# First attention of a four-block kernel: shift rows written by DMA instead of added by select matmuls, odd head moved to a step's begin

## The chip, the cores and the metric
The kernel runs on one core of a Trainium2 chip. The metric is the device time in microseconds of the whole program, the median over several executions.

## What is computed
The reference is a chain of six stages over 2048 tokens of 128 channels (8 sequences of 256): mixture of experts, attention, mixture, and once more in a second layer. The change touches the first attention alone:

```python
qkv = (x @ w_qkv.T + b_qkv).reshape(b, n, 3, H, D).transpose(2, 0, 3, 1, 4)   # H = 16, D = 8
q, k = elu(q) + 1.0, elu(k) + 1.0
q, k = _apply_rope(q, sin, cos), _apply_rope(k, sin, cos)
attn = softmax(einsum("bhnd,bhmd->bhnm", q, k) * scale, axis=-1)
out = einsum("bhnm,bhmd->bhnd", attn, v) + lepe   # lepe: a convolution of v over 3 tokens
```

With 8 sequences, 16 heads and 256 queries, each softmax row has 256 keys.

## The kernel before
**Stages.** The stages f0 (mixture), a0 (the attention of this case), g0, f1, a1 and g1 follow one another with a barrier of all engines at each stage's end (stage_end in build). In each stage every engine has a program of its own, written out by hand: sync for SP, gpsimd for POOL, tensor for PE, scalar for ACT, vector for DVE.

**Scores twice.** [...] By query (scores_by_query, L2069, and scores_by_query_paired, L2081): queries on partitions, 256 keys along the free dimension, two halves of 128 queries into one PSUM bank; DVE takes the negated maximum of it (maximum, L2292). By key (scores_by_key, L2106): keys on partitions, queries along the free dimension, into banks 2 to 5; ACT takes the exponential of two heads at once (probabilities, L2240). The negated maximum of a query has to be added to each by-key score before that.

**How it is added before.** Queries and keys are kept as a high part and a rest (three rows of 8 values = 24 rows, PARTS), and a head has 32 partitions (HW) of the turned tiles, four heads to a tile. The negated maxima of a batch are split into a bf16 high part and a rest (split_maxima, L2300), turned by PE (turn_maxima, L2096) and copied by DVE (take_shift, L2309) into a tile shift of 128 partitions. After a by-key matmul of 24 rows a second matmul of 32 rows with the 0/1 tile select adds them into the same bank.

**Order.** A batch (one sequence) has 8 steps of two heads, step n = 8 b + u. In step n PE does the by-key scores of the step's pair, and the by-query scores of the pair three steps later (LEAD = 3). The order of one step on PE: by-key of both heads, by-query of the even head, the product with V of four heads (values, in odd steps), turning of the output (turn_out, in even steps), the projection of V with its convolution (u = 5), turning of stacks (u = 1 to 4), turn_maxima (u = 6), projection of a later batch (u = 7), and at last by-query of the odd head. On DVE: split_maxima (u = 5), take_shift (u = 7), maximum of the even head, elu, finish, take_out, maximum of the odd head. Before step 0 there are 11 steps without by-key scores, and most of these do both heads in scores_by_query_paired. The last 11 steps have no by-query scores. The fp32 bank 7 (T) is used in turn by turnings of stacks, the convolution, the projection and the maxima; claim(7) waits for its last reader.

**SP in this stage.** The attention's own sync is empty. In build, SP's block then runs, for a0, fills.sync (L506: two transfers from the tile empty into the slot tables of the later mixtures, then a wait for both) and write_pads (L350: six transfers of the tile pad into z, then a wait for all).

Of the kernel before, what the change touches and what calls it, by code (L numbers as in the profile page):

```python
# [23 lines left out]
P = 128  # L24
# [377 lines left out]
class Ahead:  # L402
# [9 lines left out]
    def place(self, ctx, w):  # L412
# [9 lines left out]
        self.head = sb("head", [P, H0], BF16)  # L422
        self.select = sb("select", [P, H0, P], BF16)
# [23 lines left out]
    def constants(self, pool):  # L447
        pool.memset(self.ones_f[:, :], 1.0)
        pool.memset(self.edge[:, :, :], 0.0)
        pool.memset(self.bias_rows[:, :, :], 0.0)  # L450
        self.step(pool, pool.memset(self.head[:, :], 0.0))
# [1377 lines left out]
def attention_zero(core, name, ctx, w):  # L1829
# [11 lines left out]
    PARTS = 3 * D0  # L1841
    STEPS = H0 // 2
# [6 lines left out]
    wqkv, wv, cos, sin, ones_f, bias_rows, edge, select = (ahead.wqkv, ahead.wv, ahead.cos, ahead.sin, ahead.ones_f,  # L1849
                                                          ahead.bias_rows, ahead.edge, ahead.select)  # L1850
# [8 lines left out]
    mparts = sb("mparts", [P, 2, 4, 2 * H0], BF16)  # L1859
    shift = [sb(f"shift{i}", [P, SEQ], BF16) for i in range(2)]  # L1860
# [25 lines left out]
    shift_ready = sem("shift_ready")  # L1886
    s2_done = sem("s2_done")
# [38 lines left out]

    def group_of(n, lag):

        return (n - lag) // 2 if (n - lag) % 2 == 0 and 0 <= (n - lag) // 2 < BATCH * GROUPS else None
# [16 lines left out]
    def sync(sp):  # L1946
        pass
# [30 lines left out]
    def gpsimd(pool):  # L1978
# [6 lines left out]
        for m in stack:  # L1985
            pool.memset(m[:, :, :, :, PARTS:HW].rearrange("p a t h d -> p (a t h) d"), 0.0).then_inc(filled, 1)
# [22 lines left out]
    def tensor(pe):  # L2009
# [20 lines left out]
        def turn_stack(b, v):  # L2030
# [4 lines left out]
            if b == 0 and v == 0:  # L2035
                pe.wait_ge(filled, 3)
# [32 lines left out]
        def scores_by_query(b, h):  # L2069
            n, g, rows = b * H0 + h, h // HG, slice(HW * (h % HG), HW * (h % HG) + PARTS)  # L2070
            if h % (2 * HG) == 0:
                pe.wait_ge(tk_ready, 4 * b + 2 * (h // (2 * HG)) + 2)
            if n >= 2:
                pe.wait_ge(max_done, n - 1)
            q, k = turned[b % NT]
            for t in range(2):
                last = pe.matmul(bank[h % 2][:, SEQ * t:SEQ * t + SEQ], q[rows, g, P * t:P * t + P].bitcast(F32R),  # L2077
                                 k[rows, g, :].bitcast(F32R), start=True, stop=True)
            last.then_inc(s1_done, 1)
# [16 lines left out]
        def turn_maxima(b):  # L2096
            claim(T)
            pe.wait_ge(parts_ready, b + 1)
            for t in range(2):
                last = pe.transpose(bank[T].bitcast(BF16)[:, P * t:P * t + P],  # L2100
                                    mparts[:, t, :, :].rearrange("p i h -> p (i h)"), core.identb[:, :])
# [933 lines left out]
```

## Time and profile before

| | us |
|---|---|
| median of 3 runs | 1029.71 |
| the runs | 1030.68, 1021.74, 1029.71 |
| the profiled execution | 1020.3 |
| its span, first to last instruction | 1018.5 |
| PE busy in the span | 862.1 (85%) |
| DVE busy | 749.3 (74%) |
| ACT busy | 520.8 (51%) |

The first attention takes the stretch from about 131 to 313 us of the span. A row of the timeline gives the start, the duration, the engine, the line, the operation, the tile written and the tile read, and the number of instructions merged in the row; in brackets, the idle time before and what ended it. Windows give busy time per engine in a stretch.

### The profile page before, as it was taken

The numbers are of one execution on the slowest core, as the hardware profiler recorded it, in microseconds if no ns is written. First come the engines' busy times: TensorE is split into PE (matmuls) and PEld (weight loads), VectorE is DVE, ScalarE is ACT, GpSimd is POOL, SyncE is SP. The second block draws the span as 40 slices with busy tenths as digits, with TensorE's granted clock in tenths as the row PEclk, the third lists the DMA queues.
The fourth block names the chain that finished last, engine by engine and source line by source line (L and its number), as shares of the span: only waits on it lengthen the run. The fifth ranks groups of instructions, "written<-read, shape, count | busy, mean of one in ns | idle before, by whom it ended". The sixth has DMA issues, their size and how long they took to land.

```text
span 1018.5 us, 23321 instructions
## 1 busy us (share of the span) xinstructions
PE 862.1 (85%) x7492; PEld 655.8 (64%) x7492; DVE 749.3 (74%) x2654; ACT 520.8 (51%) x1365; POOL 284.5 (28%) x395
## 2 busy tenths in 40 slices
PE   4899989999996899945999188999999998548992
PEld 3457856667765457833999166677767776437992
DVE  7758888788767866877577658877787778566675
ACT  4233044666564223014465238877887788434653
POOL 3034035634001003117755180001000000077741
PEclk9999995999996999965899679999999999859996
DMA  9204079810006304056231256645454552343313
GB/s 238 71 1 141 1 280 374 264 52 2 2 1 161 80 1 141 1 168 187 80 84 34 84 147 194 185 123 159 149 174 139 157 155 84 92 143 90 104 36 125
DMA packets 134947, 119.74 MB, mean 118 GB/s; under 512 B 10755, under 2 KB 115227, under 8 KB 134836
## 3 DMA queue, kind: packets, MB, share of 16 engines
q1 hardware_dynamic: 130292, 109.83, 36.4%
q0 software_dynamic: 4544, 8.54, 2.5%
q8 instruction: 57, 0.93, 0.4%
q14 instruction: 54, 0.44, 0.1%
HBM read 67.45 MB, written 51.80 MB: 117 GB/s over the span
## 4 chain that ended last, share of the span: by engine, by line
PE 63%; DVE 16%; ACT 12%; issue 4%; DMA 3%; DVEq 1%; SPq 0%; POOL 0%; POOLq 0%; ACTq 0%
PE psum L955 7%; PE psum L964 6%; PE psum L1551 6%; PE psum L1465 5%; ACT a_L L2799 3%; ACT a_L L2797 3%; PE psum L2139 3%; PE psum L2669 3%; PE psum L2718 3%; PE psum L2077 3%; PE psum L2705 2%; PE psum L2042 2%; PE psum L743 2%; PE psum L1491 2%; ACT a_PT L2808 2%
## 5 line engine op out<-in xcount | busy, mean ns | idle before, releaser
L2297 DVE TENSOR_REDUCE a_negmax<-psum 128x2 f32<-128x512 f32 x128 | 83.7, 684 | 20.9 <-PE psum L2077 19.5
L2246 ACT ACTIVATE a_PT<-psum 128x1024 f32<-128x1024 f32 x64 | 65.5, 1023 | 26.2 <-PE psum L2122 25.8
L2799 ACT ACTIVATE a_L<-a_L,a_least 128x256 f32<-128x256 f32 x128 | 63.3, 495 | 0.0
L1010 ACT ACTIVATE f_hT<-psum,f_wt 128x128 f32<-128x128 f32 x156 | 44.5, 369 | 36.5 <-PE psum L955 36.5
L1010 ACT ACTIVATE g_hT<-psum,g_wt 128x128 f32<-128x128 f32 x156 | 44.4, 370 | 33.3 <-PE psum L955 33.3
L2669 PE MATMUL psum<-a_KT,a_Q 64*128 64x128 f32 (+1 forms) x512 | 57.6, 342 | 3.3 <-DVE a_least L2859 0.9
L2797 ACT ACTIVATE a_L<-a_L,a_least 128x128 f32<-128x128 f32 x128 | 50.6, 395 | 10.7 <-DVE a_least L2859 9.8
L2857 DVE CUSTOM_DVE_ANT_0 a_L<-psum,a_X 128x128 f32<-128x128 f32 x128 | 36.6, 286 | 25.0 <-PE psum L2669 24.9
L2116 PE MATMUL psum<-a_turned 24*128 24x256 f32 x256 | 53.8, 359 | 0.0
L2859 DVE CUSTOM_DVE_ANT_0 a_L<-psum,a_X 128x256 f32<-128x256 f32 x128 | 53.7, 420 | 0.0
L2808 ACT ACTIVATE a_PT<-psum 128x768 f32<-128x768 f32 x64 | 51.2, 800 | 1.7 <-PE psum L2685 0.9
L2077 PE MATMUL psum<-a_turned 24*128 24x256 f32 x224 | 51.3, 338 | 0.9 <-ACT a_turned L2212 0.7
L2685 PEld LDWEIGHTS psum<-ident,a_L 64*128 64x128 f32 x768 | 30.6, 139 | 30.7 <-ACT a_PT L2808 17.5
L2705 PE MATMUL psum<-a_PT,a_V 128*64 128x256 f32 (+1 forms) x512 | 49.9, 338 | 0.0
L163 POOL MEMSET g_logit<- 128x128 f32 x1 | 0.2, 204 | 170.7 <-DVEq L2937 170.7
L896 POOL DMA_INDIRECT g_back_dram<-g_y,g_xin x39 | 40.3, 1033 | 25.0 <-DVE g_y L1093 20.7
L896 POOL DMA_INDIRECT f_back_dram<-f_y,f_xin x39 | 39.6, 1015 | 27.5 <-DVE f_y L1093 23.6
L2122 PE MATMUL psum<-a_shift,ahead_select 32*128 32x256 bf16 x256 | 47.2, 289 | 0.0
L955 PE MATMUL psum<-f_xT,f_wt 128*128 128x128 f32 x312 | 43.4, 284 | 3.2 <-DVE f_xT L1087 3.2
L2705 PEld LDWEIGHTS psum<-a_PT,a_V 128*64 128x64 f32 x512 | 32.4, 139 | 19.7 <-issue 10.5
L2600 DVE TENSOR_SCALAR a_L<-a_L,a_rinv 128x256 f32<-128x256 f32 x128 | 44.5, 348 | 0.0
L955 PE MATMUL psum<-g_xT,g_wt 128*128 128x128 f32 x312 | 41.3, 276 | 1.9 <-DVE g_xT L1087 1.9
(579 smaller groups left out, 2563.3 us busy)
## 6 DMA issues: line engine op xcount, KB each, us to landing
z<-a_G SPq DMA_DIRECT2D x32, 512.0 KB, 3.5
a_X<-z SPq DMA_DIRECT2D x16, 1024.0 KB, 6.7
f_slots_dram<-empty SPq DMA_DIRECT2D x1, 8910.0 KB, 28.1
g_slots_dram<-empty SPq DMA_DIRECT2D x1, 8910.0 KB, 51.6
a_X<-z SPq DMA_DIRECT2D x16, 512.0 KB, 4.1
f_wgu<-in_gate_up SPq DMA_DIRECT2D x16, 384.0 KB, 6.6
z<-pad SPq DMA_DIRECT2D x6, 1024.0 KB, 9.7
g_wgu<-in_gate_up SPq DMA_DIRECT2D x16, 384.0 KB, 6.5
```

Source lines behind the costliest of these rows:

```text
L896: pool.indirect_dma_start(back_dram[:, :], bass.IndirectOffsetOnAxis(ap=xin[:, i, P:P + 1].bitcast(I32), axis=0), y[i % YBUF][:, :], None, ...
L955: last = pe.matmul(bank[i % 2][:, P * c:P * c + P], wt[i % WBUF][:, P * c:P * c + P], xT[:, i % 2, :], start=True, stop=True)
L964: last = pe.matmul(bank[4 + i % 2][:, 0:P], hT[:, i % 2, c, :], wt[i % WBUF][:, OUT + P * c:OUT + P * c + P], start=(c == 0), stop=(c == F ...
L1010: act.activation(hT[:, i % 2, c, :], bank[i % 2][:, P * c:P * c + P], ACT.Relu, bias=wt[i % WBUF][:, B1 + c:B1 + c + 1]).then_inc(relu_don ...
L2077: last = pe.matmul(bank[h % 2][:, SEQ * t:SEQ * t + SEQ], q[rows, g, P * t:P * t + P].bitcast(F32R), k[rows, g, :].bitcast(F32R), start=Tr ...
L2246: act.activation(PT[m % 4][:, :, :, :].rearrange("p j t n -> p j (t n)"), core.psum[:, 2 + 2 * (u % 2):4 + 2 * (u % 2), :], ACT.Exp, scale ...
L2297: dve.tensor_reduce(negmax[:, :, h], query_bank(b, h).rearrange("p (t n) -> p t n", n=SEQ), AX.X, ALU.max, negate=True).then_inc(max_done, 1)
L2669: last = pe.matmul(out, Q[rows, at, b % 2, queries], KT[rows, at, b % 2, keys], start=True, stop=True)
L2705: last = pe.matmul(o[D1 * i:D1 * i + D1, queries], V[s][:, kt, D1 * h:D1 * h + D1], PT[:, (2 * m + i) % TSLOTS, keys], start=(kt == 0), st ...
L2797: act.activation(pr[:, o, 0:P], L[:, o, 0:P], ACT.Exp, bias=least[:, o, 0:1], scale=-1.0, accum_out=sums[:, o, 0:1])
L2799: act.activation(pr[:, o, P:3 * P], L[:, o, P:3 * P], ACT.Exp, bias=least[:, o, 1:2], scale=-1.0, accum_out=sums[:, o, 1:2]).then_inc(p_re ...
L2808: act.activation(own.rearrange("p (k r c) -> p r k c", r=2, c=HP), core.psum[:, 2:4, 0:3 * P].rearrange("p r (k c) -> p r k c", c=HP), ACT ...
```

## The change
The select tile and its constants go. The turned queries get two more rows in use per head: rows 24 and 25 of each head's 32 hold the high part and the rest of the negated maximum, and the same rows of the keys' stack are filled with 1.0, so the by-key matmul of 26 rows adds them by itself. The rows are written by SP with eight DMAs per batch, out of a tile shift of 32 partitions in fp32r. The attention's sync now stands behind fills.sync and write_pads in SP's program. The by-query scores of the odd head are now begun at a step's begin, interleaved by halves with the by-key scores, and both maxima stand together on DVE. The turning of the maxima moves from u = 6 to 5, take_shift from the begin of u = 7 to the end of u = 5, and values_and_convolution from u = 5 to 6.

```diff
-        groups = self.head[:, :].rearrange("p (g j) -> p g j", j=HG)
-        for part in range(2):
-            self.step(pool, pool.affine_select(out=groups, in_=groups, compare_op=ALU.not_equal, fill=1.0, base=-H0 * part,
-                                               pattern=[[-HG, H0 // HG], [-33, HG]], channel_multiplier=1))
-        pool.tensor_copy(self.select[:, :, :], bcast(self.head[:, :], P))
...
-    mparts = sb("mparts", [P, 2, 4, 2 * H0], BF16)
-    shift = [sb(f"shift{i}", [P, SEQ], BF16) for i in range(2)]
+    mparts = sb("mparts", [P, 2, 2 * H0])
+    shift = [sb(f"shift{i}", [2 * H0, SEQ]) for i in range(2)]
...
-        return i + 1 if u == 5 and 1 < i + 1 < BATCH else None
+        return i + 1 if u == 6 and 1 < i + 1 < BATCH else None
...
     def sync(sp):
-        pass
+
+        for b in range(BATCH):
+            sp.wait_ge(shift_ready, b + 1)
+            for part in range(2):
+                for g in range(GROUPS):
+                    s = H0 * part + HG * g
+                    sp.dma_start(turned[b % NT][0][PARTS + part::HW, g, :],
+                                 shift[b % 2][s:s + HG, :]).then_inc(rows_written, 16)
...
-            pool.memset(m[:, :, :, :, PARTS:HW].rearrange("p a t h d -> p (a t h) d"), 0.0).then_inc(filled, 1)
+            pool.memset(m[:, 0, :, :, PARTS:HW].rearrange("p t h d -> p (t h) d"), 0.0).then_inc(filled, 1)
+            pool.memset(m[:, 1, :, :, PARTS:SHIFTED].rearrange("p t h d -> p (t h) d"), 1.0).then_inc(filled, 1)
+            pool.memset(m[:, 1, :, :, SHIFTED:HW].rearrange("p t h d -> p (t h) d"), 0.0).then_inc(filled, 1)
...
-        def scores_by_key(b, u):
+        def scores(b, u, second):
             m = b * STEPS + u
+            if second:
+                place_for_query(*second, second_order(*second))
+                by_query(*second, 0)
             if u == 0:
-                pe.wait_ge(shift_ready, b + 1)
+                pe.wait_ge(rows_written, WRITES * (b + 1))
             if m >= 2:
                 pe.wait_ge(p_ready, m - 1)
-            q, k = turned[b % NT]
             for t in range(2):
+                if second and t:
+                    by_query(*second, 1)
                 for j in range(2):
-                    h = 2 * u + j
-                    rows = slice(HW * (h % HG), HW * (h % HG) + PARTS)
-                    pe.matmul(bank[2 + 2 * (u % 2) + j][:, SEQ * t:SEQ * t + SEQ],
-                              k[rows, h // HG, P * t:P * t + P].bitcast(F32R), q[rows, h // HG, :].bitcast(F32R),
-                              start=True, stop=False, skip_group_check=True)
-                for j in range(2):
-                    h = 2 * u + j
-                    rows = slice(HW * (h % HG), HW * (h % HG) + HW)
-                    last = pe.matmul(bank[2 + 2 * (u % 2) + j][:, SEQ * t:SEQ * t + SEQ], select[rows, h, :],
-                                     shift[b % 2][rows, :], start=False, stop=True, skip_group_check=True)
+                    last = by_key(b, u, j, t)
             last.then_inc(s2_done, 1)
...
                 if n == 0:
-                    pe.wait_ge(max_done, H0 + 4)
-                scores_by_key(i, u)
+                    pe.wait_ge(max_done, H0 + 6)
+                scores(i, u, due[1])
...
-            if u == 6 and inside(i + 1):
+            if u == 5 and inside(i + 1):
                 turn_maxima(i + 1)
...
-            if due[1] and n not in PAIRED:
-                scores_by_query(*due[1])
+            if due[1] and n < PAIRED.start:
+                scores_by_query(*due[1], H0 * due[1][0] + due[1][1])
...
-            if due[0]:
-                maximum(*due[0])
+            if due[0] and n < 0:
+                maximum(*due[0], H0 * due[0][0] + due[0][1])
+            elif due[0]:
+                maximum(*due[1], second_order(*due[1]))
+                maximum(*due[0], first_order(*due[0]))
...
+            if u == 5 and inside(i + 1):
+                take_shift(i + 1)
...
             for n, st in enumerate(made):
-                st["sync"](sp)
                 if names[n] == "a0":
                     fills.sync(sp)
                     core.early.write_pads(sp)
+                st["sync"](sp)
```

Here by_query and by_key issue one matmul each (a half of 128 queries or keys, 256 columns), by_key with 26 rows; place_for_query holds the waits that scores_by_query had. first_order and second_order number the maxima in the new order (odd head first).

## Rows read from the trace of the kernel before

**Rows 1.** The page, the granted TensorE clock in 40 slices (tenths).
```profile
PEclk9999995999996999965899679999999999859996
```
**Rows 2.** Windows over the stage: window, length; busy PE, PEld, DVE, ACT, POOL; PEclk; DMA share; GB/s.
```profile
149.00:163.90 14.90, 12.88 (x72) 8.82 (x70) 13.91 (x25) 5.29 (x9) 12.16 (x19) 0.70 1.02 372
163.90:176.50 12.60, 12.60 (x88) 9.10 (x86) 9.93 (x31) 5.89 (x7) 4.03 (x15) 0.54 1.02 374
176.50:189.00 12.50, 11.81 (x133) 8.14 (x134) 10.81 (x27) 8.33 (x11) 12.27 (x17) 1.00 0.75 254
...
209.00:229.00 20.00, 19.24 (x216) 13.85 (x208) 16.16 (x39) 11.87 (x15) 7.11 (x12) 1.00 0.01 3
...
267.00:285.00 18.00, 17.68 (x210) 12.72 (x202) 14.61 (x37) 10.68 (x14) 0.00 (x0) 1.00 0.01 2
```
**Rows 3.** Timeline of SP, the time it spends on issuing DMAs.
```profile
132.31 0.68 SPq L510 DMA_DIRECT2D f_slots_dram<-empty  x1
133.04 15.67 SPq L510 DMA_DIRECT2D g_slots_dram<-empty  x1
184.71 18.11 SPq L356 DMA_DIRECT2D z<-pad  x6
...
465.83 1.41 SPq L385 DMA_DIRECT2D early_bnd<-in_b_nd  x4
```
**Rows 4.** What SP waited for, 110 to 310 us: total, times, longest.
```profile
SPq L2951 <- DMA z<-pad: 6.0, 1, 6.0
```
**Rows 5.** Timeline of PE: a pair of heads, first by-key scores, two blocks.
```profile
152.80 0.50 PE L2090 MATMUL psum<-a_turned 24*128 24x256 f32 x4
...
163.89 0.58 PE L2116 MATMUL psum<-a_turned 24*128 24x256 f32 x2
...
272.03 0.38 PE L2077 MATMUL psum<-a_turned 24*128 24x256 f32 x1
...
272.25 0.27 PE L2077 MATMUL psum<-a_turned 24*128 24x256 f32 x1
...
272.94 0.44 PE L2146 MATMUL psum<-ident,a_OT 128*128 128x128 f32 x2
...
305.55 0.39 PE L2116 MATMUL psum<-a_turned 24*128 24x256 f32 x2
...
306.24 0.44 PE L2146 MATMUL psum<-ident,a_OT 128*128 128x128 f32 x2
```
**Rows 6.** DMA issues by line: count, KB each, us from issue to landing.
```profile
g_slots_dram<-empty SPq DMA_DIRECT2D x1, 8910.0 KB, 51.6
...
z<-pad SPq DMA_DIRECT2D x6, 1024.0 KB, 9.7
...
f_wg<-in_Wg SPq DMA_DIRECT2D x1, 4.0 KB, 1.6
```
**Rows 7.** Windows at the stage's start, columns as in rows 2.
```profile
131.00:132.00 1.00, 0.53 (x2) 0.26 (x3) 0.68 (x4) 0.20 (x1) 0.52 (x1) 0.56 0.00 0
...
134.00:136.00 2.00, 1.30 (x6) 0.40 (x4) 1.70 (x10) 0.00 (x0) 0.00 (x0) 0.87 1.00 366
```
**Rows 8.** Timeline of PE and DVE, steps 5 to 7 of a late batch.
```profile
273.75 0.38 PE L2077 MATMUL psum<-a_turned 24*128 24x256 f32 x1
...
275.38 0.29 DVE L2307 TENSOR_TENSOR a_mparts<-a_negmax,a_mparts 128x128 bf16<-128x128 f32 x1
275.78 0.69 DVE L2297 TENSOR_REDUCE a_negmax<-psum 128x2 f32<-128x512 f32 x1
276.39 0.41 DVE L2327 COPY a_OT<-psum 128x256 f32<-128x256 f32 x1
...
281.33 0.28 DVE L2314 COPY a_shift<-psum 128x256 bf16<-128x256 bf16 x1
...
281.76 0.38 PE L2077 MATMUL psum<-a_turned 24*128 24x256 f32 x1
```
**Rows 9.** Timeline of POOL after the constants of the first mixture.
```profile
65.43 0.30 POOL L462 COPY ahead_wv<-ahead_wqkv 128x128 f32<-128x128 f32 x1 [56.09 <-PE psum L1438]
```

More of the change, by code:

```diff
@@ L1841, in attention_zero @@
     PARTS = 3 * D0
+    SHIFTED = PARTS + 2
     STEPS = H0 // 2
@@ L1847, in attention_zero @@
     T, VB = 7, 6
-    wqkv, wv, cos, sin, ones_f, bias_rows, edge, select = (ahead.wqkv, ahead.wv, ahead.cos, ahead.sin, ahead.ones_f,
-                                                          ahead.bias_rows, ahead.edge, ahead.select)
+    wqkv, wv, cos, sin, ones_f, bias_rows, edge = (ahead.wqkv, ahead.wv, ahead.cos, ahead.sin, ahead.ones_f,
+                                                  ahead.bias_rows, ahead.edge)
     e = [sb(f"e{i}", [P, 4, P]) for i in range(2)]
@@ L1886, in attention_zero @@
     shift_ready = sem("shift_ready")
+    rows_written = sem("rows_written")
     s2_done = sem("s2_done")
@@ L1925, in query_bank, with second_order, first_order @@
         return bank[(3, 5)[h % 2]] if n in PAIRED and n % 2 == 0 else bank[h % 2]
+    def second_order(b, h):
+        n = b * H0 + h
+        return n - 1
+    def first_order(b, h):
+        n = b * H0 + h
+        return n if (n // 2 - STEPS - LEAD) < 0 else n + 1
     def group_of(n, lag):
@@ L2067, in values_and_convolution, with place_for_query, by_query, by_key @@
             release[i] = (l_added, b + 1)
-        def scores_by_query(b, h):
-            n, g, rows = b * H0 + h, h // HG, slice(HW * (h % HG), HW * (h % HG) + PARTS)
-            if h % (2 * HG) == 0:
+        def place_for_query(b, h, order):
+            if h % (2 * HG) in (0, 1):
                 pe.wait_ge(tk_ready, 4 * b + 2 * (h // (2 * HG)) + 2)
-            if n >= 2:
-                pe.wait_ge(max_done, n - 1)
+            if order >= 2:
+                pe.wait_ge(max_done, order - 1)
+        def by_query(b, h, t):
+            g, rows = h // HG, slice(HW * (h % HG), HW * (h % HG) + PARTS)
             q, k = turned[b % NT]
+            last = pe.matmul(bank[h % 2][:, SEQ * t:SEQ * t + SEQ], q[rows, g, P * t:P * t + P].bitcast(F32R),
+                             k[rows, g, :].bitcast(F32R), start=True, stop=True)
+            if t:
+                last.then_inc(s1_done, 1)
+        def by_key(b, u, j, t):
+            h = 2 * u + j
+            g, rows = h // HG, slice(HW * (h % HG), HW * (h % HG) + SHIFTED)
+            q, k = turned[b % NT]
+            return pe.matmul(bank[2 + 2 * (u % 2) + j][:, SEQ * t:SEQ * t + SEQ], k[rows, g, P * t:P * t + P].bitcast(F32R),
+                             q[rows, g, :].bitcast(F32R), start=True, stop=True)
+        def scores_by_query(b, h, order):
+            place_for_query(b, h, order)
             for t in range(2):
-                last = pe.matmul(bank[h % 2][:, SEQ * t:SEQ * t + SEQ], q[rows, g, P * t:P * t + P].bitcast(F32R),
-                                 k[rows, g, :].bitcast(F32R), start=True, stop=True)
-            last.then_inc(s1_done, 1)
+                by_query(b, h, t)
         def scores_by_query_paired(b, h):
@@ L2290, in elus, with maximum @@
                                      ALU.add).then_inc(elu_ready, 1)
-        def maximum(b, h):
-            n = b * H0 + h
-            dve.wait_ge(s1_done, n + 1)
-            if h == 0 and b:
+        def maximum(b, h, order):
+            dve.wait_ge(s1_done, order + 1)
+            if h in (0, 1) and b:
                 dve.wait_ge(parts_ready, b)
@@ L2312, in take_shift @@
             if b >= 2:
-                dve.wait_ge(s2_done, STEPS * (b - 1))
-            dve.tensor_copy(shift[b % 2][:, :], bank[T].bitcast(BF16)[:, 0:SEQ]).then_inc(shift_ready, 1)
+                dve.wait_ge(rows_written, WRITES * (b - 1))
+            dve.tensor_copy(shift[b % 2][:, :].bitcast(F32R), bank[T][0:2 * H0, 0:SEQ]).then_inc(shift_ready, 1)
         def add_convolution(b):
@@ L2372, in vector @@
                 add_convolution(value_step(n - 1))
-            if u == 7 and inside(i + 1):
-                take_shift(i + 1)
-            if due[0]:
-                maximum(*due[0])
+            if due[0] and n < 0:
[3 more added lines that the diff above has]
+                maximum(*due[0], first_order(*due[0]))
             if n in (-6, 0):
@@ L2384, in vector @@
                 take_out(group_of(n, 3))
-            if due[1]:
-                maximum(*due[1])
+            if due[1] and n < 0:
+                maximum(*due[1], H0 * due[1][0] + due[1][1])
+            if u == 5 and inside(i + 1):
+                take_shift(i + 1)
     return dict(sync=sync, gpsimd=gpsimd, tensor=tensor, scalar=scalar, vector=vector)
```

21 lines of the change are left out of this document (8 added, 13 removed).

## The prediction
> **What bounds the kernel now.** I read the profile from coarse to fine. The 40 slices (25.5 us each) come first: the granted TensorE clock is at 0.9 of full speed or more in most, and at 0.5 in the seventh, 153 to 178 us, which belongs to this stage [rows 1]. The windows over the stage come second [rows 2]. They say that the stage, 131 to 313 us, is carried by PE: it is busy 19.24 of 20.0 us in an early batch (209 to 229) and 17.68 of 18.0 in a late one (267 to 285). DVE is next, with 16.16 of 20.0 and 14.61 of 18.0. So an edit that frees PE gains at once, but only until DVE, 2 to 3 us per batch behind, takes over. The same windows hold what decides this case: from 149 to 189 us, and on until the pads have landed, the 16 DMA engines are full (share 1.02 until 176.5, then 0.75 with the gap at 184 in it, 254 to 374 GB/s), and after 209 they are empty. Third, SP's own timeline and waits [rows 3, 4]. In the kernel before SP has nothing to do for the attention, so it sends the two fills at 132.31 and 133.04, waits until the second has landed (133.04 + 51.6 = 184.6 [rows 6]), sends the six pads until 202.8, and waits 6.0 us for them. Nobody waits for SP in this, since the stage runs to 313 us. Fourth, the block of the scores on PE, instruction by instruction [rows 5].
>
> **The changed place of SP's work: the stall.** The first scores by key begin at 163.89 us [rows 5]. In the changed kernel they need the shift rows written by DMA (step 0 of PE waits on rows_written), and these DMAs stand in SP's program behind fills.sync and write_pads, each of which ends with a wait for its own transfers. SP is free at 184.71 + 18.11 + 6.0 = 208.8 us [rows 3, 4]. Nothing in the change makes the fills shorter: they move 2 x 8.9 MB and 6 x 1 MB through full engines [rows 2, 6]. Then come eight DMAs of 4 KB. SP issued four small ones (5 KB each) in 1.41 us, 0.35 each [rows 3]; the eighth starts 7 x 0.35 = 2.5 us after the first. A lone 4 KB load landed 1.6 us after its issue [rows 6]. With 0.1 for SP to come out of its wait: 208.8 + 0.1 + 2.5 + 1.6 = 213.0 us. **The first step is late by 213.0 - 163.9 = 49.1 us.** Bounds: nothing shows an SBUF to SBUF transfer. Large issues take 0.47 each and the fill's rate could differ by 1 us, so 48 to 52.
>
> Does other work fill the stall? Behind the waiting PE stands everything of the attention. Before it waits, PE does one matmul of a by-query score; the second half of it comes after the first by-key matmuls, so s1_done does not rise, the maximum on DVE waits, behind it DVE's statistics and the elu of batch 3, and so POOL. ACT waits for s2_done. Nothing that is on the path later can be done early, so I subtract nothing. The barrier at the stage's end moves the rest of the program by the same time.
>
> **Clock after the stall.** Behind the barrier at the stage's start, where PE was busy for 0.53 of 1 us, the clock was 0.56, and 3 us later 0.87; from 163.9 to 176.5 it was 0.54, although PE was busy throughout [rows 2, 7]. [...] I take 0. [...]
>
> **The additions by select.** A step's block before: four by-query matmuls (two heads, two halves), four by key, four by select. It ran from 272.03 to 272.94 = 0.91 us [rows 5]. Without queries, as in the last 11 steps, four by key and four by select took 306.24 - 305.55 = 0.69 us [rows 5]. Four matmuls of 24 rows in two row groups showed 0.50 us from start to end [rows 5], with the second pair 0.22 behind the first and some 0.28 of latency; so the pitch of one row group is 0.22 and the pair costs 0.44. The changed block has eight matmuls in four row groups: odd query and two keys together, then their second halves at 0.22, and the even head's two, which can start beside them at 0.22 and 0.44: 0.66 us. If only two row groups ran at once it would be 4 x 0.22 = 0.88; if all four did it would be 0.44. I take 0.66, because the block before also holds more than two at a time. Saved: 0.25 per step with queries, 0.69 - 0.44 = 0.25 per step without. [...]
>
> There are 53 steps with queries: 53 x 0.25 = 13 us. DVE limits it: a maximum takes 0.69 us, 0.6 behind one another, two per step [rows 8], and a late batch has 14.61 us of DVE in 18.0, with little slack in the steps that have no turning of stacks. I count three quarters: 10 us (bounds 2 and 18). The 11 last steps: 11 x 0.25 = 2.7 us, nothing else binds there.
>
> **The rows of batches 1 to 7.** The split now stands with the turning in step 5 and the result must be in place at step 8. Take a late batch, step 5 beginning at 273.75 [rows 8]. The split ended at 275.67 (+1.9). DVE then does two maxima (1.2), the copy of O (0.4) and take_shift (0.3): +3.8 [rows 8]. Eight DMAs: +2.5, landing +1.6: +7.9. The next batch began at 281.76, +8.0 [rows 8]; with three shorter blocks PE would be there at +7.3. So a wait of 0.6 us in three late batches (the others have a projection in step 7), 2 us together; at 0.47 an issue and 2.5 us of landing it would be up to 1.8 in seven, 12 us. This DMA chain is why steps 5 to 7 gain almost nothing in the late batches. What is queued behind: the convolution of step 6 claims bank 7, which take_shift frees at +3.8; the split at 128x128 and the bf16 copy get smaller operands, less than 0.5 us per batch of DVE, counted with the three quarters.
>
> **Small edits.** Head and select vanish from POOL's constants in the first mixture, where POOL afterwards idles 56 us before its next piece [rows 9]: 0. Four more memsets and the wait at H0 + 6 lie ahead of step 0 and are covered by the stall: 0. Without that cover the wait would cost one maximum, 0.7.
>
> **Sum.** 1020.3 + 49.1 (stall) - 10 - 2.7 (blocks) + 2 (rows) + 0 (clock) = 1058.7 us, against the profiled execution. Its 1020.3 stands 9.4 below the median of three runs; the four executions shown average 1025.6. I put the same +38.4 on that: 1064 us.
>
> **Rivals.**
> - *Rows become a chain of their own* (7 in 100): issue and landing at their upper bounds, so each batch waits 1.8 us and half the blocks' gain goes: 1025.6 + 51 - 6 + 12 = 1083. For it: the slack of 0 in the late batches. Against: small DMAs show 0.35 and 1.6.
> - *The whole gain comes through* (20 in 100, among the 92 of the forecast): block at 0.44, DVE no limit: 53 x 0.47 x 0.75 = 19, so 1025.6 + 49 - 19 - 2.7 + 1 = 1054.
> - *Faster, since step 0 isn't held* (1 in 100): it decides from the moment SP is free by about 170 us, for then stall and gain cancel. The price of the stall would be 0 and the time 1025.6 - 10.7 = 1015. It needs the fills and pads, 24 MB, to be through 39 us sooner; the rows show the engines full, so nothing speaks for it except that SP's waits are read from code.
> - *The change does little*: stall and gain both small, within 1% (2 in 100): SP would have to be free near 175 to 185 us.
>
> **How the numbers follow.** The forecast with its variants (92 in 100) gives 1064, with its own range from 1025.6 + 48 - 21 - 2.7 = 1050 to about 1080 (stall 52, blocks 5, rows 6, clock +2). The range 1050 to 1082 leaves out the slow tail of the first rival and the two small ones. One per cent is about what a measurement of this kernel can tell from no change: slower by over that 0.96, within 0.02, faster 0.02.
>
> **What the profile after should show.** SP's eight DMAs of batch 0 begin at about 209 us and PE and DVE are empty from 164 to 213; no matmul reads select; the block takes 0.66 us; the stage from resumption to barrier is near 149 - 11 = 138 us against 149. Wrong would be: DMAs of the rows before 200 us, a block of 0.88, or PE waiting more than 1 us for rows in each batch.

## The result, and the profile after

The changed kernel takes 1078.62 us (median of 4 runs, 1076.05 to 1081.36) against 1028.61 for the kernel before (4 runs): a ratio of 1.0506, 95% interval 1.0458 to 1.0554. It is 50 us slower; 38 were forecast.

The stall is where the forecast put it. SP's timeline of the changed kernel (start, duration; the last row is from a narrower window):

```profile
131.63 0.68 SPq L502 DMA_DIRECT2D f_slots_dram<-empty  x1
132.37 15.68 SPq L502 DMA_DIRECT2D g_slots_dram<-empty  x1
183.10 17.29 SPq L356 DMA_DIRECT2D z<-pad  x6
...
206.84 4.52 SPq L1957 DMA_DIRECT2D a_turned<-a_shift  x8
```

They answer [rows 3]. The fills and pads run as before, and the first row DMA of the attention is issued at 206.84 us, although the maxima of batch 0 were ready some 45 us earlier. The chain of work that ended last, between 205 and 216 us (start, duration, what):

```profile
196.76 10.06 DMA z<-pad
...
206.84 0.68 SPq L1957
...
210.87 1.62 DMA a_turned<-a_shift
...
212.53 0.58 PE psum L2102 x2
```

The first by-key matmul, at 163.89 us in [rows 5], stands at 212.53. PE's waits say it too (total, times, longest):

```profile
PE psum L2102 <- DMA a_turned<-a_shift: 47.8, 4, 45.2
```

One wait of 45.2 us, and 2.6 us over three later ones (3.9 over six if PE's weight loads are counted, the longest 1.3). So once SP is free the eight small DMAs cost each batch little.

What follows the stall was expected to be shorter than before and is longer. From the first by-key matmul to the next stage's first DMA (312.91 us before, 372.97 after) it is 149.0 us before and 160.5 after. Windows of the changed kernel over that stretch (window, length; busy PE, PEld, DVE, ACT, POOL; granted clock; DMA share; GB/s):

```profile
212.50:225.50 13.00, 11.87 (x73) 7.93 (x73) 9.19 (x27) 6.91 (x8) 5.96 (x17) 0.50 0.00 1
225.50:250.00 24.50, 20.67 (x194) 11.96 (x192) 18.10 (x43) 13.65 (x18) 16.71 (x24) 0.86 0.01 2
250.00:338.60 88.60, 81.05 (x767) 52.19 (x766) 68.72 (x162) 48.24 (x62) 21.11 (x30) 0.92 0.01 3
338.60:355.80 17.20, 16.57 (x111) 9.82 (x111) 9.54 (x27) 6.23 (x7) 0.00 (x0) 0.51 0.01 3
355.80:373.00 17.20, 13.27 (x149) 7.05 (x147) 6.92 (x25) 10.75 (x12) 0.00 (x0) 1.00 0.01 2
```

The column to read is the clock, 1.00 in both late rows of [rows 2] (209 to 229 and 267 to 285). Here it is 0.50 for the first 13 us, 0.51 for 17 us in the last batch, and 0.92 in between. In windows of 1 us it is at 1.00 or at 0.50, but for those in which it changes; the two are called full clock and lower level from here on. The 0.92 is made of short falls of 3 to 4 us, one at each batch's begin, such as this one:

```profile
300.00:301.00 1.00, 0.54 (x8) 0.43 (x12) 0.93 (x3) 0.47 (x1) 0.98 (x1) 0.84 0.00 0
301.00:302.00 1.00, 1.00 (x12) 0.27 (x4) 1.00 (x3) 0.00 (x0) 1.00 (x2) 0.50 0.00 0
302.00:303.00 1.00, 1.00 (x8) 0.72 (x4) 0.90 (x2) 0.00 (x0) 0.92 (x3) 0.50 0.00 0
303.00:304.00 1.00, 1.00 (x11) 0.57 (x9) 0.00 (x0) 0.60 (x1) 1.00 (x1) 0.50 0.00 0
304.00:305.00 1.00, 1.00 (x11) 0.83 (x12) 0.97 (x2) 0.92 (x2) 0.94 (x3) 0.95 0.00 0
```

Counted in windows of 1 us, the clock is at the lower level for some 51 us between the first and the last by-key matmul, against 12 in the kernel before. The blocks of the scores, where nothing holds them up, are shorter than forecast. PE's timeline of two blocks of the changed kernel, and DVE's row just before the even head's pair of the first:

```profile
288.68 0.39 PE L2102 MATMUL psum<-a_turned 26*128 26x256 f32 x2
...
289.27 0.47 PE L2093 MATMUL psum<-a_turned 24*128 24x256 f32 x2
289.67 1.07 PE L2162 MATMUL psum<-a_PT,a_Vs 128*32 128x256 f32 x16
...
294.53 0.38 PE L2093 MATMUL psum<-a_turned 24*128 24x256 f32 x1
294.54 0.39 PE L2102 MATMUL psum<-a_turned 26*128 26x256 f32 x2
294.55 0.48 PE L2093 MATMUL psum<-a_turned 24*128 24x256 f32 x2
...
294.98 1.07 PE L2162 MATMUL psum<-a_PT,a_Vs 128*32 128x256 f32 x16
```
```profile
287.84 1.29 DVE L2319 TENSOR_REDUCE a_negmax<-psum 128x2 f32<-128x512 f32 x2 [0.48 <-PE psum L2093]
```

The second block, with all eight matmuls in four row groups, takes 294.98 - 294.53 = 0.45 us. The first takes 0.99: the even head's pair starts at 289.27, 0.59 behind the others. The only wait that place_for_query leaves open there is that for DVE's maxima, and DVE's two maxima end at 287.84 + 1.29 = 289.13, just before; so the delay is DVE's. The profile itself names no releaser there.

The short block isn't the usual one. Of 39 blocks with queries between 243 and 338 us (from a block's first matmul to PE's next other matmul, clock 0.92 on average) 12 took 0.44 to 0.45 us, 15 took 0.95 to 1.07, and 5, in the first two steps of a batch, 1.56 to 1.93. The mean is 0.88. In the kernel before, 48 blocks between 176 and 288 us had a mean of 0.97, and 37 of them took 0.91 to 0.93.

### The profile page after: what moved, and what is told of

It reads as the page before. It is cut to its first block, busy times and chain, and to the rows that moved or that the text cites. A ratio compares the mean times of both kernels' runs of the same rounds, so it can differ in the third digit from the quotient of the medians.

```text
span 1074.3 us, 22893 instructions
## 1 busy us (share of the span) xinstructions
PE 862.0 (80%) x7236; PEld 643.0 (60%) x7236; DVE 750.7 (70%) x2654; ACT 518.3 (48%) x1365; POOL 283.7 (26%) x395
## 4 chain that ended last, share of the span: by engine, by line
PE 52%; DVE 15%; ACT 13%; issue 5%; SPq 5%; DMA 4%; another core or an unknown queue 3%; POOL 1%; DVEq 1%; POOLq 0%; ACTq 0%
PE psum L947 6%; PE psum L956 6%; PE psum L1543 5%; PE psum L1457 4%; ACT a_L L2822 3%; ACT a_L L2820 3%; PE psum L2162 3%; PE psum L2741 3%; PE psum L2692 3%; PE psum L2093 2%; ACT a_PT L2831 2%; PE psum L2728 2%; PE psum L1483 2%; SPq L502 2%
## 5 line engine op out<-in xcount | busy, mean ns | idle before, releaser
L2102 PE MATMUL psum<-a_turned 26*128 26x256 f32 x256 | 36.3, 366 | 47.8 <-DMA a_turned<-a_shift 47.8
L2820 ACT ACTIVATE a_L<-a_L,a_least 128x128 f32<-128x128 f32 x128 | 50.6, 396 | 10.7 <-DVE a_least L2882 9.8
L2102 PEld LDWEIGHTS psum<-a_turned 26*128 26x128 f32 x256 | 21.9, 211 | 52.1 <-DMA a_turned<-a_shift 49.4
L2093 PE MATMUL psum<-a_turned 24*128 24x256 f32 x224 | 46.8, 365 | 7.7 <-DVE a_negmax L2319 5.3
L2162 PE MATMUL psum<-a_PT,a_Vs 128*32 128x256 f32 x512 | 41.8, 452 | 3.5 <-DVE a_attn L2357 2.1
L2093 PEld LDWEIGHTS psum<-a_turned 24*128 24x128 f32 x224 | 29.1, 211 | 25.8 <-issue 13.5
## 6 DMA issues: line engine op xcount, KB each, us to landing
z<-pad SPq DMA_DIRECT2D x6, 1024.0 KB, 10.1
```

What stands on the lines that cost most here:

```text
L2162: last = pe.matmul(bank[VB][VW * j:VW * j + VW, 0:SEQ], Vs[b % NT][:, t, HG * g + j, :], PT[(2 * m + j // 2) % 4][:, j % 2, t, :], start=( ...
L2820: act.activation(pr[:, o, 0:P], L[:, o, 0:P], ACT.Exp, bias=least[:, o, 0:1], scale=-1.0, accum_out=sums[:, o, 0:1])
```

## The measure used from here on

The experiments change both the work of the stretch and the clock during it. To tell the two apart I multiply the stretch from the first to the last by-key matmul by its mean granted clock. The product is an estimate of mine: the length at a granted clock of 1.00 throughout, if PE set the pace everywhere and its pace went with the clock. (PE is busy for 0.89 to 0.97 of the stretch; the idle rest is counted at the same mean clock, so the product is a measure of PE's work and its waits together.) How far it holds is seen where the work is the same: the two traces of the kernel before, at clocks of 0.96 and 0.90, come to 137.4 and 138.3 us (below). The kernel before, then the changed one:

```profile
163.90:307.00 143.10, 139.41 (x1502) 98.74 (x1500) 110.83 (x278) 85.27 (x103) 43.68 (x70) 0.96 0.29 95
```
```profile
212.50:367.00 154.50, 140.25 (x1245) 87.55 (x1245) 109.86 (x271) 83.24 (x103) 43.79 (x70) 0.84 0.01 3
```

143.1 x 0.96 = 137.4 us before, 154.5 x 0.84 = 129.8 us after. The clock is given to two digits, so the product is good to 0.8 us. Each product rests on one profiled execution.

The same rows, by the same estimate, give PE's busy time alone at full clock: 139.4 x 0.96 = 133.8 us before, 140.25 x 0.84 = 117.8 after, so 16 us of work have gone. But PE is idle for 14.3 us of the stretch instead of 3.7. Most of the difference between the 16 us and the 7.6 by which the products differ is this idle time.

## The experiments

The experiments ran on four chips, on each beside the kernel before. The chips differed by up to 4%: the kernel before took 1066.55 us (median) on the chip of the first four runs, 1025.89 on that of the next four, 1068.14 on that of the next three (fillers ahead of step 0) and again 1068.14 on that of the last one (the order alone). Whole times are therefore compared only as ratios to the kernel before on the same chip. The difference between the chips lies behind this stage: from the next stage's first DMA to the end it is 701 to 708 us in the six traces of the faster chips and 738 to 745 in the eight of the slower ones. Stretches inside the stage can be compared across chips.

### Is the place of SP's work the whole stall?

**Rows first.** The attention's sync stands ahead of the fills again:

```diff
             for n, st in enumerate(made):
+                st["sync"](sp)
                 if names[n] == "a0":
                     fills.sync(sp)
                     core.early.write_pads(sp)
-                st["sync"](sp)
```

> The changed kernel with the attention's own sync ahead of the fills and pads again, so that the rows of batch 0 can be written at about 161 us; the fills and pads (24 MB) then come after the last rows, near the stage's end. Theory S (the place of SP's work is the whole stall): the first by-key matmuls come at about 166 us instead of 212.5, PE is never idle for more than 4 us, and the attention's last PE instruction comes at 166 + 150..160 = 316 to 326 us; then the barrier waits for fills and pads, some 76 us, so the whole time is 1020 + 75 + 0..12 = 1095 to 1110. Rival (the rows are late for a reason of their own, contention or the transfer itself): the first by-key matmuls later than 175 us. For the rest of the loss: if it is only the clock after the 48 us gap, the stretch from first by-key matmul to last PE instruction falls from 160 to 149 or less; if it is the order and the waits for rows, it stays above 152.

Measured, in one execution: first by-key matmul at 167.8 us, 1131.48 us in all. SP's timeline of this run shows the rows from 162.06 us and the fills after them, at the stage's end:

```profile
162.06 150.83 SPq L1957 DMA_DIRECT2D a_turned<-a_shift  x64
312.94 0.66 SPq L502 DMA_DIRECT2D f_slots_dram<-empty  x1
313.64 16.05 SPq L502 DMA_DIRECT2D g_slots_dram<-empty  x1
```

So 44.7 of the 48.6 us come from the place in SP's program. The other 3.9 (2.5 against the second trace of the kernel before, below) remain with SP free: from the first of the eight DMAs to the first by-key matmul it is 5.7 us. The whole time was above the expected 1095 to 1110, but on a slower chip, which adds some 35 us behind the stage. The second question has an answer as well: the stretch is 155.5 us long (167.8 to 323.3), as long as after a 48 us gap, at a mean clock of 0.81. So the lower clock of this stretch isn't a consequence of the gap.

**Rows by ACT.** The rows of batches 0 to 2 are issued from ACT's own queue, and SP does fills and pads first:

```diff
+    BY_ACT = 3
...
+        for b in range(BY_ACT, BATCH):
+            write_rows(sp, b)
...
                 probabilities(i, u)
+            if u == 6 and 0 <= i + 1 < BY_ACT:
+                write_rows(act, i + 1)
```

> The changed kernel with the rows of batches 0, 1 and 2 issued by ACT (its own DMA queue, behind its work of step 6), SP keeps fills and pads first and the rows of batches 3 to 7. Theory S: the stall goes, the first by-key matmuls come at 166 to 170 us, the whole time is 1078.6 - 46 + 2..6 (ACT busy with issuing eight DMAs in batches 1 and 2, rows landing between the packets of the fills) = 1033 to 1040, near or a little above the kernel before. Rival 1 (the rows queue behind the fills whatever engine issues them, since the 16 DMA engines are full): first by-key matmuls at 184 us or later, time above 1050. Rival 2 (once the stall is gone the removal of select shows its gain): below 1020.

Measured: ratio 1.0222 (1.0192 to 1.0251), first by-key matmul at 179.3 us. That is between the theory and its first rival, and the trace shows a third thing. ACT's timeline while the fills and pads are under way (the rows at 164 and 198 us, DMA share 1.02 and 0.94), and after them (225 us, share 0.03):

```profile
164.41 10.14 ACTq L1955 DMA_DIRECT2D a_turned<-a_shift  x8
174.60 0.60 ACT L2240 ACTIVATE a_turned<-psum 128x512 fp32r<-128x512 f32 x1 [9.60 <-issue]
...
198.19 9.22 ACTq L1955 DMA_DIRECT2D a_turned<-a_shift  x8
...
225.34 4.58 ACTq L1955 DMA_DIRECT2D a_turned<-a_shift  x8
```

Issuing the eight DMAs took 10.1 and 9.2 us at those shares and 4.6 at 0.03, and ACT's other work stands behind it. The last row DMA of batch 0 was issued by 174.6 us, the first by-key matmul came 4.8 us later. So the rows didn't wait for the end of the fills (184 us), but they were slow (3.5 us of PE's wait for batch 0, 4.6 for batch 1) and held up their issuer; after the first one PE waits for rows 7.5 us more, over four waits, against 2.6 in the changed kernel.

**Dealt out.** SP does rows of batch 0, a quarter of the fills, rows of batch 1, the next quarter, and so on; the pads follow the rows of batches 4 and 5, and all waits stand at the end:

```diff
+                    core.fill_part = lambda sp, b: (fills.part(sp, b) if b < 4 else
+                                                    core.early.write_some(sp, b - 4) if b < 6 else None)
                 st["sync"](sp)
+                if names[n] == "a0":
+                    fills.wait_all(sp)
+                    core.early.wait_pads(sp)
```

> The changed kernel with SP's order dealt out: rows of batch 0, a quarter of the two fills, rows of batch 1, the next quarter, and so on, three pads behind the rows of batches 4 and 5 each, all waits for fills and pads at the end. Theory S (the place of SP's work is the stall): first by-key matmuls at 166 to 168 us, no long gap, whole time 45 to 49 us below the changed kernel on the same chip, so a ratio of 1.000 to 1.010 to the kernel before. The forecast's step on the blocks (11 us gained): ratio 0.990. Theory C (the clock): in this kernel too some 50 us of the attention at the lower clock against 20 before, and from the first by-key matmul to the stage's end 153 to 162 us.

Measured: ratio 1.0119 (1.0075 to 1.0163). First by-key matmul at 168.8 us. This removes 38.7 thousandths of the 50.6, some 40 us (the two intervals leave 33 to 46). Theory S said 45 to 49; in the traces the first by-key matmul comes 43.7 us earlier than in the changed kernel. Some 10 us are left (1.0119; medians 1035.1 against 1025.89). Of these 3.5 to 4.9 are still the rows' own way, by which the first by-key matmul is later than in the two traces of the kernel before (163.9 and 165.3); the rest must lie behind it. The stretch, from this kernel's windows:

```profile
168.80:318.00 149.20, 135.65 (x1242) 85.42 (x1241) 109.83 (x271) 82.50 (x103) 43.77 (x70) 0.87 0.48 167
```

149.2 x 0.87 = 129.8, the same as in the changed kernel, with 39 us at the lower clock. Theory C had expected some 50, and 153 to 162 us to the stage's end; it was 155.6.

### Does the clock after the stall matter?

**Warm stall.** PE computes on ones while it would wait:

```diff
+                if n == 0:
+                    for _ in range(215):
+                        pe.matmul(bank[2], core.ones[:, :], some, start=True, stop=True)
                 scores(i, u, due[1])
```

> The changed kernel with 215 matmuls of ones (128x512, bf16) on PE, into a bank that is free, while it would wait for the rows of batch 0: 46 us of work at the higher clock in a gap of 48. Theory C (the cold clock after the stall costs most of what the forecast missed, about 11 us in batch 0): granted clock 1.0 at the first by-key matmuls, batch 0 shorter by 6 to 11 us, whole time 1067 to 1073 against 1078.6. Rival (the clock is low for what the steps themselves do, whatever came before): the clock falls again within batch 0, gain 0 to 3 us, time 1075 to 1079.

Measured: ratio 1.0527 (1.0495 to 1.0558), not below the 1.0506 of the changed kernel. The windows show that the filler did what it should (213 fillers in 45.0 us, 0.21 us each), and that it was no use:

```profile
175.00:220.00 45.00, 43.56 (x213) 20.00 (x211) 2.88 (x8) 2.42 (x3) 0.00 (x0) 1.00 0.65 204
220.00:222.00 2.00, 1.46 (x9) 1.15 (x10) 1.93 (x12) 0.81 (x2) 0.00 (x0) 0.50 0.00 0
222.00:238.00 16.00, 15.19 (x102) 8.69 (x106) 10.61 (x25) 7.94 (x10) 14.38 (x29) 0.50 0.01 3
```

Clock 1.00 for 45 us of fillers, and 0.50 from some 4 us after the by-key steps begin (216.5 us), for some 20 us (the rows show 18). By-key steps began 4.0 us later than in the changed kernel, so the stretch is what counts, and it is no shorter: 156.1 us against 154.5. The rival stands as far as this goes: keeping PE busy beforehand didn't keep the clock up in the steps. What in the steps lets it fall, the run doesn't say. 156.1 x 0.83 = 129.6.

### Is it the clock that takes the blocks' gain away?

**The kernel before again.**

> The kernel before, unchanged, for its trace on the same chip as the next three. [...]

I expected what the first trace shows: one low stretch of some 20 us, and 149 us from the first by-key matmul to the stage's end. That was wrong, and usefully so. One execution gave 159.9 us from the first by-key matmul to the stage's end (165.3 to 325.2). The same code has a second low stretch here, from 190 to 210 us:

```profile
189.00:209.00 20.00, 19.31 (x133) 12.19 (x132) 11.61 (x25) 8.90 (x11) 7.59 (x11) 0.54 0.95 285
```

Where the first trace shows 220 matmuls in this window at clock 1.00, this one has 133 at 0.54. The run took 1031.45 us, 11 more than the first profiled execution. From the first by-key matmul to the stage's end the difference is 159.9 - 149.0 = 10.9 us. So 20 us more at the lower level cost 10.9 us in one and the same kernel, and it is at least one cause of the spread of the kernel before between 1021 and 1031. By the product, 153.7 x 0.90 = 138.3: the same work as in the first trace.

**One and two fillers a step.** Dealt out as above, with matmuls that compute nothing at the begin of each step (one, and six at a batch's first step; then two and eight):

```diff
+            if m >= 2:
+                pe.wait_ge(p_ready, m - 1)
+                for _ in range(6 if u == 0 else 1):
+                    pe.matmul(bank[2 + 2 * (u % 2)], core.ones[:, :], some, start=True, stop=True)
```

> e5_dealt_out with matmuls that compute nothing: one of 128x512 bf16 at the begin of each step, six at each batch's first step, ahead of the wait for the rows. They add 64 x 0.21 + 8 x 1.1 = 22 us of work to PE. Theory C (the clock falls because PE has less work in its steps once select is gone, and each fall costs more than the work saved): fewer than 25 us at the lower clock, the stretch 4 to 10 us shorter than in e5, although PE does more. Rival (PE and DVE time alone decide): the same or up to 10 us longer than e5.

> As e6_filler_one with two at each step and eight at a batch's first: 64 x 0.43 + 8 x 1.3 = 38 us of work added. Theory C: the clock is high throughout after the first steps; the time as e6 or up to 5 us above it, since PE is then full. Rival: 15 to 25 us above e5.

Measured: ratios 1.0096 (1.0058 to 1.0133) and 1.0145 (1.0101 to 1.0188). The stretches, first with one filler a step, then with two:

```profile
168.90:319.00 150.10, 141.88 (x1340) 86.15 (x1340) 109.10 (x271) 85.55 (x103) 43.69 (x70) 0.96 0.48 166
```
```profile
168.00:325.60 157.60, 151.06 (x1411) 88.51 (x1411) 110.30 (x273) 86.02 (x103) 43.76 (x70) 0.98 0.46 158
```

The clock part of theory C holds: all falls after 180 us are gone (clock 1.00 from 181 us to the stretch's end in both), 12 and 7 us at the lower level instead of 39. The time part holds by half: the stretch with 14 us more of work in it (150.1 x 0.96 = 144.1 against 129.8) lasts 150.1 us against 149.2. It isn't shorter by the 4 to 10 us expected. What the clock gives back the filler eats; the intervals of the whole-time ratios 1.0119 and 1.0096 overlap. With two fillers the stretch is 7.5 us longer than with one and 8.4 longer than without, between theory C (0 to 5 above one) and its rival (15 to 25 above none). The expectations counted 22 and 38 us of filler; the products rise by 14 and 25, so part of the filler went into time in which PE was idle.

### Can the first low stretch be prevented?

The kernel before and two of the above, with three fillers in each of the eight steps ahead of step 0; "dealt out" also with five at a batch's first step:

```diff
+                for _ in range(3):
+                    pe.matmul(bank[T if n < -4 else 4], core.ones[:, :], some, start=True, stop=True)
```

> The kernel before, with three matmuls that compute nothing (128x512 bf16, 0.64 us together at the higher clock) at the begin of each of the eight steps ahead of step 0 in which PE waits for maxima. [...] Rival: the clock falls anyway, and the added 5 us of work come on top: 0 to 5 us longer.

> e5_dealt_out with the same early matmuls and five more at the first step of each batch (ahead of the wait for the rows), none in the other steps: 5 + 8 us of work. Theory C: fewer than 15 us at the lower clock, ratio to the kernel before 0.990 to 1.000, and 8 to 15 us less than e5_dealt_out had. Rival (fillers at the batches' begins alone don't hold the clock, since the steps of the changed kernel are thin everywhere): falls as in e5, ratio 1.005 to 1.015.

> e6_filler_one with the same early matmuls. Theory C: no low stretch left but a few us, ratio 1.000 to 1.005 (e6 had 1.0096; the low stretch at the first steps is worth 5 to 9 us). Rival: 1.010 or more.

Measured: 1.008 (1.0037 to 1.0123), 1.005 (1.0016 to 1.0084), 1.0058 (1.0027 to 1.009), in this order. For the kernel before, theory C wanted a clock at the full level, or falling later and for less time, and 4 to 9 us less. The clock was 1.00 until 169 us, and then it fell all the same, twice, to 0.50 for some 23 and 21 us. The rival stands: nothing gained, the work on top. With the changed steps, the early fall moved from 155 to 164 and 169 us and lasted 17 and 14 us (clock 0.50 and 0.51), followed by shorter ones; "dealt out" was at the lower level for 25 us of the stretch, where theory C wanted fewer than 15 and a ratio of 1.000 or less. Their ratios are lower than without the early fillers, but on another chip and with intervals that touch; I count it as not shown. What makes the long falls of 14 to 27 us, in which PE is busy for 0.77 to 1.00 of the time, stays open. The last one of the changed kernel, at 338 us, comes 1 us after a gap of PE, and the short ones mostly follow gaps too (window, length; busy PE, PEld, DVE, ACT, POOL; granted clock; DMA share; GB/s):

```profile
336.00:337.00 1.00, 0.03 (x1) 0.00 (x0) 0.52 (x2) 0.00 (x0) 0.00 (x0) 1.00 0.03 8
```

But a gap isn't enough: in the kernel before, PE was busy for 0.51 and 0.55 us of the microseconds from 186 and 247 us, at clock 1.00, and no fall followed.

### Which part of the change is worth something?

**Old order, select gone.** Rows first, with the by-query scores of the odd head and the maxima put back to their old places.

> As e1_rows_first, with the order of the by-query scores and of the maxima put back: odd head at a step's end, both on PE and on DVE. Theory O (two maxima together on DVE make the even head's by-query scores wait, which gives the gain of the block away): the stretch from first by-key matmul to the last PE instruction is 3 to 8 us shorter than that of e1. Rival (the new order is what lets the scores run four at a time, and gains): the stretch is 3 to 8 us longer than in e1. Neither: within 2 us.

Measured: 159.4 us from first to last by-key matmul against 155.5, at clocks of 0.82 and 0.81, so 130.7 against 126.0. By that the new order is worth 4.7 us, and the stretch itself is 3.9 us shorter. My theory O, that two maxima in a row on DVE cost more than they give, is refuted. The size is less sure: it is one execution each, and the 126.0 stands 3.6 to 3.9 below the other products of its kind in the table below.

**The order alone.** The kernel before with the new order and nothing else of the change:

```diff
+            if second:
+                place_for_query(*second, second_order(*second))
+                by_query(*second, 0)
             if u == 0:
                 pe.wait_ge(shift_ready, b + 1)
...
             for t in range(2):
+                if second and t:
+                    by_query(*second, 1)
```

> The kernel before with only the order of the change: the odd head's by-query scores at a step's begin, both maxima together on DVE; select matmuls, the shift by PE and copy, the place of the turning and SP's program as before. Counted so far over the stretch from the first to the last by-key matmul, less half of the time at the lower clock: 137 us for the kernel before (three traces), 129 for the changed one (five traces), and 126 against 131 for the changed one with new and old order. Theory (the order is worth about 4 of the 8 us by itself, and with select in place PE's steps are full enough that the clock makes no short falls): 131 to 134 by that count, no falls of 3 us, ratio 0.992 to 0.998. Rival (the order gains only where select is gone, since the two additions fill the place): 136 to 139, ratio 1.000 or more. Rival (the clock falls in short stretches with the new order as well, since it packs the work closer and leaves gaps behind): falls of 3 us as in the changed kernel, ratio 1.002 or more.

Measured: ratio 0.9949 (0.9921 to 0.9977): half a per cent faster than the kernel before, clear of noise, and the only kernel here that is. Its stretch:

```profile
165.70:309.00 143.30, 136.17 (x1500) 94.20 (x1500) 109.72 (x274) 85.07 (x103) 43.64 (x70) 0.93 0.28 90
```

143.3 x 0.93 = 133.3 against 137.4: 4.1 us less. The clock has one short fall of 4 us after the long one at the start (27 us here, from 155 us), where the changed kernel has six and a second long one. PE is idle for 7.1 us of this stretch, against 14.3 in the changed kernel. Counted in windows of 1 us at full clock, PE is busy for less than 0.65 us in 4 windows here, in 2 and 3 in the two traces of the kernel before, and in 11 in the changed one. That fits the theory that select in place keeps the steps full. It isn't shown: the changed kernel's gaps at the batches' begins are made of waits for the rows (up to 1.1 us), for maxima (0.4), and for others (0.5), the kernel with the order alone has no row DMAs, and no run has select gone without them.

The same comparison prices the rest of the change. Rows by DMA and select gone, dealt out so that SP holds nobody up, stand at 1.0119; the order alone at 0.9949.

## The products side by side

| kernel | stretch, us | mean clock | product |
|---|---|---|---|
| before, first trace | 143.1 | 0.96 | 137.4 |
| before again | 153.7 | 0.90 | 138.3 |
| before, early fillers | 159.1 | 0.86 | 136.8 |
| order alone | 143.3 | 0.93 | 133.3 |
| changed | 154.5 | 0.84 | 129.8 |
| changed, warm stall | 156.1 | 0.83 | 129.6 |
| changed, rows by ACT | 162.4 | 0.80 | 129.9 |
| changed, dealt out | 149.2 | 0.87 | 129.8 |
| changed, rows first | 155.5 | 0.81 | 126.0 |
| changed, rows first, old order | 159.4 | 0.82 | 130.7 |
| dealt out, early fillers, five at batch begins | 151.0 | 0.92 | 138.9 |
| dealt out, one filler | 150.1 | 0.96 | 144.1 |
| dealt out, two fillers | 157.6 | 0.98 | 154.4 |
| dealt out, one filler, early fillers | 152.3 | 0.95 | 144.7 |

But for "rows first", stretches of the same work differ by up to 16 us, their products by 1.5 us or less. That is the best evidence that their lengths differ with the granted clock and not by a wait. Between the changed kernel and the kernel before, the clock is 19 us of the stretch (154.5 x 0.16 - 143.1 x 0.04), against 7.6 gained. "Rows first" is below the others of its kind by 4 us; in it, and in its twin with the old order, no fills or pads run beside the steps or just before them. I didn't follow that up.

## Why the prediction was right, and where it was not

- **The stall** (49.1 us forecast). Right, 48.6 us, and by the steps named: SP is held by the fills and pads. Two terms were off by little, and it is luck that they cancelled: SP was free at 206.8 instead of 208.8, a DMA of the rows takes 0.54 us to issue (0.50 and a gap of 0.04) instead of 0.35, so the eighth started 4.0 us after the first; and it landed in 1.62 us, as forecast from the lone 4 KB load of [rows 6] (1.6).
- **Nothing fills the stall.** Right: from 164 to 212 us PE is busy 1.7 of 48 us.
- **The blocks** (10 + 2.7 us gained). Right in kind and nearly in size, at equal clock: 137.4 - 129.8 = 7.6 us with the 2.6 us of row waits in it, so 10 us against 12.7. PE's work shrank by 16 us, as much as the 13 + 2.7 of the full count, and more of it than the quarter set aside for DVE came back as idle time. A free block takes 0.45 us (294.53 to 294.98), near the 0.44 that the forecast gave for four row groups at once and set aside for 0.66; the more frequent one takes about 1.0, because the even head's pair waits for DVE. So the 0.66 of the forecast is neither, and that the gain comes out near is in part luck. Of the gain, some 4 us belong to the order (4.1, and less surely 4.7) and the rest to select's removal.
- **The rows of batches 1 to 7** (2 us lost). Right: 2.6 us, the longest 1.1.
- **The clock** ("I take 0"). This is the term that failed. No run shows a term of 0, nor the 2 us of clock in the upper end of the range; the runs showed a cost of some 20 us in its place, by the count below. The forecast looked at the clock near the stage's start and around step 0 alone, and added nothing for the rest of the stage. The rows had a hint against it: 0.70 from 149.0 to 163.9 us means that the fall came some 9 us ahead of step 0, with no barrier near. In the changed kernel the clock is at the lower level for 51 us instead of 12. By the two traces of the kernel before, 20 such us cost 10.9, so 39 more cost about 20. The sum then closes against the profiled execution: 48.6 - 10 + 2.6 + 20 = 61 by terms, 60 by the trace (212.5 - 163.9 + 160.5 - 149.0 = 60.1); everything after this stage took 4.3 us less (701.3 against 705.6), which I didn't look into.
- **The base.** The first profiled execution of the kernel before was a lucky one, with one low stretch; the forecast had added 5.3 us for that. Against the second trace (159.9 us from first by-key matmul to stage's end) the changed kernel's 160.5 is no longer, so against a usual run the blocks' gain is eaten up rather than turned into a loss, and the 50.0 us between the medians are near the 48.6 of the stall. That they agree proves little: dealt out, without the stall, the change still loses some 10 us.
- **The range.** The 1078.6 us lie inside 1050 to 1082, but 14.6 above the forecast of 1064. The upper end was built from a longer stall, a smaller gain, longer row waits and 2 us of clock. The time got there by some 20 us of clock, which was not in it. That it still lies inside is luck.
- **Slips in the working.** The chances of the forecast and its rivals (92, 7, 1 and 2 in 100) add up to 102. With the upper bounds for issue and landing the wait for rows is 3.8 + 3.3 + 2.5 - 7.3 = 2.3 us a batch and not 1.8. DVE stands 3.1 us behind PE in both windows of [rows 2], not 2 to 3 per batch. None of them moves the sum.

Four things are seen of the clock and not explained: it was 1.00 during the 45 us of fillers of the warm stall; the short falls (3 to 4 us) mostly came behind gaps of PE; they were gone with a filler in each step (1.00 from 181 to 319 us); and the long falls came with PE at work, in one of them for 19.3 of 20 us at 0.54. No run here shows what the long falls depend on.

## What to carry to other kernels

Before moving an engine's transfers behind others in its program, read what that engine waits for and until when, in its own timeline; a queue that held nobody up becomes the path with one new wait. Work taken off TensorE can come back as idle time and as time at the lower clock (here 16 us of work less, 10 us more idle, 39 us more at the lower level), so a gain of a few per cent there is to be counted as length times granted clock, and the clock looked at apart. And a change with several parts should be timed in parts: here the one part that pays, the order, was hidden under one that cost 40 to 49 us.

## What the runs showed of the hardware

- The same kernel on the same inputs had one fall of the clock to 0.50 for some 20 us in one trace (from 155 us, PE busy 17.3 of the 18.0 us from 156) and two in the other (from 156 and 191 us, PE busy 18.2 and 19.0 of 19.0 us from 157 and 191). The second fall came with 10.9 us more from the first by-key matmul to the stage's end.
- Eight DMAs of four partitions by 1 KB, SBUF to SBUF, took 4.3 to 4.6 us to issue from SP or ACT at a DMA share of 0.02 to 0.08, and 10.1 and 9.2 us from ACT at 1.02 and 0.94, while fills and pads were under way.
- Eight fp32r matmuls of 24 or 26 rows and 256 columns, spread over four row groups, took 0.45 us from the first one's start to PE's next other matmul, at clock 1.00 (changed kernel, 294.53 us); four in two row groups took 0.50 from start to end [rows 5].
